# Adding the two halves of the rotated queries on VectorE ahead of the transposition

## What is computed

```python
x = x + gat_two_layers(ctx, layernorm(x))     # attention over a graph, 8 heads, masked by layernorm(x)
x = x + ffn_block(layernorm(x))               # the part that the change touches:
    q = rmsnorm((h @ q_w.T).reshape(B, S, 16, 128), q_norm_w)
    k = rmsnorm((h @ k_w.T).reshape(B, S, 4, 128), k_norm_w)
    q, k = apply_rope(q, cos, sin), apply_rope(k, cos, sin)
    # apply_rope: concat([x1 * c - x2 * s, x2 * c + x1 * s])
    hidden = hidden + causal_attention(q, k, v) @ o_w.T
    hidden = hidden + mixture_of_8_experts(rmsnorm(hidden))
```

## Time and profile before

| what | value |
|---|---|
| median of three runs | 677.07 us (676.18 to 681.5) |
| span of the profiled execution | 676.1 us |
| TensorE busy | 604.8 us, 89% |
| VectorE busy | 441.0 us, 65% |
| GpSimd busy | 292.0 us, 43% |
| ScalarE busy | 266.7 us, 39% |
| mean granted clock of TensorE | 0.944 |

### The profile page before, as it was taken

The page is one execution under the profiler, slowest core; times in us unless marked ns, Lnnn a source line. Parts: engine busy times, 40 slices in busy tenths (PEclk is TensorE's granted clock), DMA queues, the critical chain, the costliest instruction groups (busy, mean ns, idle before and its releaser), DMA issues.

```text
span 676.1 us, 11574 instructions
## 1 busy us (share of the span) xinstructions
PE 604.8 (89%) x3140; PEld 445.9 (66%) x3140; DVE 441.0 (65%) x1277; ACT 266.7 (39%) x653; POOL 292.0 (43%) x588
## 2 busy tenths in 40 slices
PE   2786938979999998879999998879999998999998
PEld 1573933559678873558778973458777974676786
DVE  5727537975738756985738765986738766565363
ACT  2313305546533304636633304647633303674020
POOL 1514325885424023886425023886424126773000
PEclk9997558898999998979999998989999999999999
DMA  8900000000000000000000000000000000000000
GB/s 313 380 6 0 2 16 4 1 2 1 0 1 2 2 26 10 4 0 2 0 1 1 1 26 10 1 0 1 1 1 1 1 1 16 1 1 1 1 1 16
DMA packets 8305, 14.51 MB, mean 21 GB/s; under 512 B 860, under 2 KB 7068, under 8 KB 7988
## 3 DMA queue, kind: packets, MB, share of 16 engines
q1 hardware_dynamic: 8244, 13.76, 5.8%
HBM read 12.70 MB, written 1.05 MB: 20 GB/s over the span
## 4 chain that ended last, share of the span: by engine, by line
PE 56%; DVE 16%; issue 13%; POOL 9%; ACT 4%; POOLq 1%; DMA 1%; DVEq 0%; ACTq 0%; SPq 0%
PE bank L565 10%; PE bank L463 9%; PE ob L443 9%; PE bank L523 5%; PE tb L432 5%; PE bank L542 4%; DVE tt L904 3%; POOL m L775 2%; PE bank L538 2%; PE bank L534 2%; PE bank L509 2%; DVE lr L895 2%; PE zb L424 1%; ACT prob L666 1%; PE zb L414 1%
## 5 line engine op out<-in xcount | busy, mean ns | idle before, releaser
L735 POOL TENSOR_SCALAR tt<-tt,gmn 128x256 f32<-128x256 f32 x128 | 77.1, 613 | 64.1 <-DVE gmn L904 63.5
L509 PE MATMUL bank<-wqkv_sb,hT 128*128 128x512 f32 x192 | 97.9, 648 | 0.0
L666 ACT ACTIVATE prob<-bank,sneg,rms 128x128 f32<-128x128 f32 (+1 forms) x128 | 64.0, 507 | 68.5 <-DVE sneg L995 67.7
L775 POOL TENSOR_TENSOR m<-early,rope_s 128x256 f32<-128x256 f32 x80 | 70.8, 908 | 42.1 <-ACT early L647 41.8
L463 PE MATMUL bank<-m,wgu_sb 128*128 128x128 f32 (+1 forms) x480 | 86.6, 330 | 1.0 <-DVE m L1025 0.6
L791 POOL TENSOR_SCALAR prob<-prob,srcp 128x128 f32<-128x128 f32 (+1 forms) x128 | 53.7, 436 | 55.5 <-DVE srcp L1066 55.4
L463 PEld LDWEIGHTS bank<-m,wgu_sb 128*128 128x128 f32 x480 | 71.2, 191 | 9.2 <-issue 2.2
L443 PEld LDWEIGHTS ob<-feat,gpT 128*128 128x128 f32 x512 | 75.8, 227 | 0.8 <-issue 0.6
L443 PE MATMUL ob<-feat,gpT 128*128 128x33 f32 x512 | 75.2, 297 | 0.0
L895 DVE SCALAR_TENSOR_TENSOR lr<-zs 128x512 f32<-128x512 f32 x64 | 50.9, 797 | 25.3 <-ACT zs L625 22.6
L904 DVE CUSTOM_DVE_ANT_0 tt<-lr,maskv 128x256 f32<-128x256 f32 x128 | 62.3, 522 | 3.5 <-issue 2.9
(11 more groups left out here) (151 smaller groups left out, 1026.5 us busy)
## 6 DMA issues: line engine op xcount, KB each, us to landing
wqkv_sb<-wqkv_dram SPq DMA_DIRECT2D x1, 3072.0 KB, 12.4
wgu_sb<-wgu_dram SPq DMA_DIRECT2D x2, 1408.0 KB, 11.2
wo_sb<-wo_dram SPq DMA_DIRECT2D x1, 2048.0 KB, 17.8
wd_sb<-wd_dram SPq DMA_DIRECT2D x1, 1408.0 KB, 15.6
xin<-x_dram SPq DMA_DIRECT2D x4, 256.0 KB, 2.7
out_dram<-rows SPq DMA_DIRECT2D x8, 128.0 KB, 1.9
rows<-gat_rows_dram SPq DMA_DIRECT2D x1, 512.0 KB
cst<-consts_dram SPq DMA_DIRECT2D x1, 425.0 KB, 3.6
```

The costliest lines, as they stand in the source:

```text
L509: mm = pe.matmul(ps[:, :], hT[:, k, t * P:(t + 1) * P], wqkv_sb[:, k, c * G * HD:(c + 1) * G * HD], start=(k == 0), stop=(k == KT - 1))
L666: ins = act.activation(prob[:, n % 5, i * nk:(i + 1) * nk], ps[:, i * nk:(i + 1) * nk], ACT.Exp, bias=sneg[:, n, i:i + 1], scale=rq(g, t, ...
L735: ins = pool.tensor_scalar(tt[:, k % 3, h, :], tt[:, k % 3, h, :], -1.0, gmn[:, k % 3, h:h + 1], ALU.mult, ALU.add)
L775: ins = pool.tensor_tensor(dst[:, :, c, :], src[:, :, 1 - c, :], s_, ALU.mult)
```

## The change

VectorE adds `m2` to `m1` in place for each query block, in a new function `rope_sums`, as it did for the keys. A table `ROPE_AT` puts the sum of block u two steps or one behind the block's products and one step ahead of its transposition; within the step it stands behind all pieces of the step (`use(s)`) and ahead of the second norm and the reciprocals. TensorE waits for the sum by a new semaphore `rope_ready` and transposes once, 4 instructions in place of 8. GpSimd may overwrite `m2` when the sum of block u - 4 is done (for blocks 4 and 5: when the keys are ready), no longer when that block is transposed.

```diff
+ROPE_AT = (7, 8, 9, 10, 10, 11, 12, 13)
...
+assert all(QKV_AT[n + 4] < ROPE_AT[n] < TURN_AT[n + 2] for n in range(len(ROPE_AT)))
...
@@ TensorE, waits ahead of a block @@
                     else:
-                        pe.wait_ge(m1_ready, b * QU + n + 4)
-                        pe.wait_ge(m2_ready, b * QU + n + 4)
+                        pe.wait_ge(rope_ready, b * len(ROPE_AT) + n - 1)
@@ TensorE, the block @@
-                        if n < T:
-                            mm = pe.transpose(dst, m1[:, n % 4, src], ident)
-                        else:
-                            pe.matmul(dst, m1[:, n % 4, src], ident, is_transpose=True, start=True, stop=False)
-                            mm = pe.matmul(dst, m2[:, n % 4, src], ident, is_transpose=True, start=False, stop=True)
+                        mm = pe.transpose(dst, m1[:, n % 4, src], ident)
@@ GpSimd, the sine products @@
-                    if u >= 4:
-                        filled(pool, b, ("turn", u - 4))
+                    if u >= 6:
+                        pool.wait_ge(rope_ready, b * len(ROPE_AT) + u - 5)
+                    elif u >= 4:
+                        pool.wait_ge(k_ready, (b + 1) * T)
@@ VectorE @@
+            def rope_sums(b, s):
+
+                for u in [n + 2 for n, at in enumerate(ROPE_AT) if at == s]:
+                    dve.wait_ge(m2_ready, b * QU + u + 4)
+                    dve.wait_ge(m1_ready, b * QU + u + 4)
+                    dve.nop(nofuse=True)
+                    dve.tensor_tensor(m1[:, u % 4, :], m1[:, u % 4, :], m2[:, u % 4, :], ALU.add).then_inc(rope_ready, 1)
...
                     for w in use(s):
                         part(b, w)
+                    rope_sums(b, s)
                     second_norm(b, s)
                     reciprocals(b, s)
```

More of the change, by code:

```diff
@@ L288, in block_program @@
         free = [sem(f"free{k}") for k in range(BANKS)]
-        raw_ready, m1_ready, m2_ready = sem("raw_ready"), sem("m1_ready"), sem("m2_ready")
+        raw_ready, m1_ready, m2_ready, rope_ready = sem("raw_ready"), sem("m1_ready"), sem("m2_ready"), sem("rope_ready")
         k_ready, seed_ready, rms_ready, pool_b = sem("k_ready"), sem("seed_ready"), sem("rms_ready"), sem("pool_b")
@@ L1194, in _ @@
                     part(B - 1, w)
+                rope_sums(B - 1, s)
                 second_norm(B - 1, s)
```

## The result

The changed kernel takes **700.23 us** (median of 4 runs, 694.01 to 700.4), the kernel before 679.29 us beside it: **1.0287 times the time, interval 1.0246 to 1.0328**. It is slower, as forecast, but by 2.9% where 1.7% was forecast, and it lies above the range of 679 to 698 us. The profiled execution took 700.13 us; its span is 698.3 us, 22.2 more than the 676.1 of before, where the sum said 11.3.

What follows compares the result with a forecast made beforehand. VectorE and its chain were taken to bound the kernel to about 306 us, TensorE behind. Passes of 0.9, 2.5 and 2.5 plus 5.4 us in the last batch gave +11.3 us, about 688 us, 1.7% slower; range 679 to 698.

Steps and rivals of the forecast that it cites:

- What bounds the kernel: VectorE and its chain with GpSimd and ScalarE decide from about 270 to 306 us; TensorE begins to decide at blocks 7 to 9.
- The waits: TensorE idles for VectorE's sums before blocks 2, 3, 7, 8, 9: 4 to 5 us at 2, 2 to 3.5 at 7.
- the lost idle time at block 6: TensorE's old idle time of 3.94 us before block 6 is used up by the new waits.
- First maximum: VectorE's maximum over scores 0 comes 1.4 us later in a pass, with three sums standing ahead of it.
- Blocks 5 and 6: Both sums, 1.3 us together, hide in VectorE's idle 2.42 us behind the first maximum; cost nothing.
- Blocks 7 to 9: New round trip of scores, maximum, sum and next block: +2.25 us, taken as +2.5 with the clock, second and third pass each.
- First pass: First loop pass: 2.5 us less 1.6 us it had already lost, mostly to a fallen clock; +0.9 us.
- Last batch: No other layer runs beside it, so the round trip at blocks 7 to 9 is bare; +5.4 us, including 1.5 for the clock.
- A gain: Rival: sums always ahead of TensorE, so savings where it decides count in full, 7.4 us; 669.7 us, 4%.
- hidden waits: Rival: the new waits overlap with slack counted as used; a pass costs -0.65 us, about 679 us in all, 20%.
- The lasting clock ahead of the first scores: Rival: clock stays down from block 2 to the first scores, 3 us more per pass; 697 us, 8%.
- the collisions: Rival: VectorE's sums collide with GpSimd, up to 0.48 us more each; 10 us, or 5 with half hit, 693 us; 12%.

Runs made afterwards that it cites:

- Half the transposes: Kernel before with one transpose per query block, nothing added on VectorE and no new wait, sine products left out of the scores; 679.76 us, 0.9991.
- waits without sums: The change's waits and single transposes, but VectorE only counts up the semaphore at each sum's place; 690.01 us, 1.0137.
- blocks 2 to 6: The change for query blocks 2 to 6 alone; 7, 8 and 9 keep two transposes and the waits of before; 690.64 us, 1.0151.
- busy wait, more: The change, TensorE kept busy by identity transposes before blocks 2, 3, 7 in the loop and 7, 8, 9 in the last batch; 692.95 us, 1.019.
- blocks 7 to 9: The change for query blocks 7, 8 and 9 alone; 2 to 6 keep two transposes and have no sum; 689.29 us, 1.0168.
- busy wait: The change, with identity transposes on TensorE: 40 before block 2 in the loop, 28 before block 7 everywhere; 696.57 us, 1.0264.
- unused sums: Kernel before with the eight sums on VectorE at the change's places, into a tile nobody reads, TensorE as before; 691.71 us, 1.0168.

## Why the prediction was right in direction and too small

**What bounds the kernel: right, with one line drawn in the wrong place.** VectorE and ScalarE decide ahead, TensorE behind. The forecast put block 7 on TensorE's side ("blocks 7, 8 and 9 lie where it begins to decide, 3 x 0.44 = 1.3 us per pass"). Half the transposes alone gave 0.9991: the line is ScalarE's copy at 306.35 us, behind scores 2. A row with an idle time of 0.35 us named ScalarE there, and a TensorE at 88.4 of 89 us from 306 us on the earlier trace rows had hidden it.

**The waits: right at blocks 2 and 7**, in place, length and releaser, and the lost idle time at block 6 too. Blocks 8 and 9 have waits in the last batch, as forecast; in the second pass half clock makes TensorE come too late to wait there, and with the clock held it waits 1.09 and 0.43 us.

**First maximum, forecast +1.4, measured +2.1: mis-sized.** The three sums cost VectorE what was reckoned: 1.44 us where TensorE is left alone. The rest is a step left out. The product of block 7 stands just ahead of the maximum, and its projection is queued on TensorE behind the waits for the sums of blocks 2 and 3; VectorE waits 0.97 us for it. With the clock held the first maximum is at 24.39, so 0.34 of the 2.1 us are clock.

**Blocks 5 and 6, "cost nothing": nearly right.** They filled the gap of 2.42 us; the second maximum is 2.33 late, 0.2 more than the first. That delay, forecast 1.4, goes on to TensorE in full: 0.9 us per pass too little.

**Blocks 7 to 9: the step that failed is the clock.** "The second makes block 7 and scores 2 about twice as long, of which the round trip shows some 0.5 us", of which 0.25 us stayed in the term. Half clock lasted 9.7 us, not the three of the earlier trace rows, and held over the whole round trip, where nothing hides it. Held at full clock, the kernel gains 10.59 - 7.66 = 2.9 us between the second and the fourth maximum in the second pass, and 2.7 in the third (10.38 - 7.67). The trace of the kernel before had a longer fall to go by: behind its stall of 3.94 us at block 6 TensorE worked at half clock for five microseconds.

```profile
297.90:302.90 5.00, 4.96 (x18) 3.58 (x19) 4.90 (x11) 1.96 (x4) 4.19 (x7) 0.50 0.00 0
```

The trip itself is right: the stretch is 0.7 us longer than before at full clock (7.66 against 6.96), forecast 0.85. Of the 10.9 us by which the forecast's sum was short, this clock makes some 5; the later second maximum makes 1.8, the first pass 1.4, the last batch 1.0, and what follows 2.1.

**Second pass, 2.1 us behind the maximum of scores 5: not forecast; they go with the clock.** The clock fell at 380 us, some 108 us into the pass, where the same pass of the kernel before has no fall, and stayed down for some 7 us from 421, where that pass has a fall of some 4. In the profiled executions six passes have a fall that starts 104 to 108 us into the pass, and each is 1.3 to 3.1 us longer behind the maximum of scores 5 than the same pass before: the second of the change, of "waits without sums", "blocks 2 to 6" and "busy wait, more", and the third of "blocks 7 to 9" and "busy wait". The third pass of the change has none and loses nothing there. What sets such a fall off no run shows.

**First pass, +0.9 forecast, +2.25 measured.** Here the second and the fourth maximum are both 2.3 later. The argument that the pass had already lost its 1.6 us held for the clock, not for VectorE's path: the 1.4 was struck out with it.

**Last batch, +5.4 forecast, +6.4 measured: right in kind.** Its second maximum is 1.4 us late (24.80 against 23.40), which the forecast had at nothing; with more of the clock held it is 5.1.

**The rivals.** A gain and hidden waits did not come. The lasting clock ahead of the first scores came in two experiments, not in the change. On VectorE the collisions were small. The sums of the changed kernel, durations in ns as least, median, greatest:

```profile
L1067 DVE TENSOR_TENSOR m<-m x32: 674/691/1291, 126.7 to 620.0; 128x512 f32<-128x512 f32 x32
```

Against a mean of 767 ns that is 32 x 0.076 = 2.4 us in all, where the rival had 5 to 10. The longest took nearly twice the median. GpSimd pays more, and the rival had priced VectorE's side alone. Its sine products with sums and no waits, then with waits and no sums:

```profile
L780 POOL TENSOR_TENSOR m<-early,rope_s x80: 717/904/1247, 104.9 to 606.2; 128x256 f32<-128x256 f32 x80
L782 POOL TENSOR_TENSOR m<-early,rope_s x80: 717/727/1248, 104.9 to 604.2; 128x256 f32<-128x256 f32 x80
```

All of GpSimd's 588 instructions take 305.5 us in the one and 292.3 in the other, 305.0 in the change and 292.0 before. So the sums lengthen GpSimd's work by 13 us. In the change VectorE's sums waited 1.4 us in all for GpSimd; how much of the 13 us lies on the path no run shows. The page SBUF — State Buffer of the Trainium skill, section "SBUF: two separate sides", has a VectorE operation with two SBUF inputs and a GpSimd operation that reads SBUF exclude each other, which fits both rows; no run isolates it.

## What to carry to other kernels

Ask of a removed instruction which engine ends the wait right behind it: a row with a few tenths of idle time that names another engine is a warning that the saving may turn into a longer wait there, as it did here, however busy the engine looks. Where a change makes the matrix engine stall, price the clock behind the stall by what is then on the path, in each pass, and not by the shortest fall in the trace. And a late operation on one engine stalls others even where nobody waits for that operation: with sums that no one read, TensorE stood still for 5.37 us at one block in place of 3.94, and the kernel lost 1.7%.

## What the runs showed of the hardware

**A fall of the clock lasts unequally long.** 3 us, 6.3 and 9.7 us in the change, the last with TensorE busy for 9.23 of them. It can also come with no idle time ahead. The change, TensorE's busy time and clock in two neighbouring stretches:

```profile
379.00:380.00 1.00, 1.00 (x12) 1.00 (x10) 0.85 (x5) 0.57 (x3) 0.83 (x2) 1.00 0.00 0
380.00:381.00 1.00, 1.00 (x6) 1.00 (x6) 0.97 (x6) 0.41 (x1) 0.38 (x1) 0.52 0.00 0
```

The matmuls there are small: outputs of 33 and 8 columns, and half the number fits into a microsecond after the fall. The same matmuls run at full clock in that pass of the kernel before.

**The granted clock can be recorded wrongly.** Ahead of the first pass, TensorE's projections in the kernel before and then in the kernel with unused sums, which does the same there:

```profile
100.21 3.78 PE L509 MATMUL bank<-wqkv_sb,hT 128*128 128x512 f32 x4
...
105.62 5.42 PE L509 MATMUL bank<-wqkv_sb,hT 128*128 128x512 f32 x12
```

```profile
100.27 3.78 PE L512 MATMUL bank<-wqkv_sb,hT 128*128 128x512 f32 x4
...
106.32 7.04 PE L512 MATMUL bank<-wqkv_sb,hT 128*128 128x512 f32 x12
```

The first four take the same 3.78 us, half speed; the clock from 99.5 to 104 us reads 0.50 in the one and 1.00 in the other. The twelve behind took 5.42 and 7.04 us: full speed came later in the second, and its first pass starts 2.3 us later for it. This is one way in which single executions come to differ; experiments were compared by their medians and by times inside a pass. The page TensorE: Matmul & The Clock Gate of the Trainium skill, section "Seeing it yourself", says that such records have been seen to be unreliable, and this case agrees.

**A count-up without an operation runs ahead on VectorE.** In the kernel with waits and no sums, block 2 started at 281.45 us without a wait, although VectorE had yet to start the products that stand ahead of that count in its order, at 284.32 us. The same place with a sum released TensorE only at 284.74, in a pass that had started 1.6 us earlier.
